# Loop order on TensorE: one V projection ahead of the values calls, one turn of queries behind a projection

## The chip, the cores and the metric

One NeuronCore of a Trainium2 chip runs the whole program. The metric is device time in microseconds of one execution; before the change it is 2621.0 us, the median of three runs.

## The reference

Eight sequences of 1024 tokens with 128 channels pass through a "macaron" block: half a local transformer, full causal attention, half the same local transformer again, each with a layer norm ahead and a residual around it.

```python
x = x + 0.5 * ffn(layernorm(x), ...)
x = x + attn(layernorm(x), Wk, Wq, Wv)
x = x + 0.5 * ffn(layernorm(x), ...)
```

`ffn` has two layers. Each shifts half of the channels by one token, projects to queries, keys and values of 8 heads of 64, normalises queries and keys and rotates them, attends in windows of 64 keys plus the 64 before them, projects back, and then applies a layer norm and a gated feed-forward of 341 hidden units, both with residuals. So local layers run four times in all over every token, and full attention once.

## The kernel before

The work of a local layer is cut into turns of 256 tokens, t = 0 to 127 over the four layers (32 a layer, 64 a phase; phase 0 lies ahead of the full attention and phase 1 behind it). Each turn has two halves i = 0, 1 of 128 tokens. Its steps on TensorE are: `project(t, i, x)`, three matmuls of 512 columns for x = Q, K or V (lines 619 to 621); `turn(t, i, x)`, four transposes of the rotated queries or keys (line 628); `scores(t, i)`, the mask (line 644) and 16 small products of queries and keys (line 652) for score groups 2i and 2i + 1; `turn_p(t, g)`, four transposes of the weights of group g (line 662); `values(t, i)`, 16 products of values and weights (line 678); `wo`, the output projection (lines 690 to 692). Two turns make a pair u, and the feed-forward works on pairs: `turn_rows` (line 701), `turn_back` (718), `to_gate` and `to_up` (723 to 725), `down` (742). `turn_ln` (756) exists in layers 0 and 2 only, `turn_y` (766) in layers 1 and 3 only.

Each engine has its own list of calls, written out by hand. In the middle of each phase the list is a loop, `local`, whose round s issues calls of several turns at different stages, with t = 2s; phase 0 runs s = 9 to 31 and phase 1 runs s = 41 to 62, 45 rounds together. Other engines serve these calls: ScalarE squares projections (line 4395), copies turned queries (4419) and values (4430), takes exponentials group by group (`exp_rows`, 4440, four ACTIVATE with a read of the sum behind each), copies turned weights (4447) and copies the outputs of the values calls (`split_o`, 4454, once for each half). VectorE takes row maxima and rotates, GpSimd adds, scales and normalises.

Results of TensorE lie in eight PSUM banks, each shared by several uses. `ROTA` lists the users of each bank in the order of a round, as (name, lag): the call of turn 2s - lag (or pair s - lag). `FIRST_USERS` and `LAST_USERS` hold the same for the calls outside the loop. From these lists each use gets the one before it in its bank, and `vacant` makes a TensorE call wait until that one has been emptied:

```python
        def vacant(on, what, n):
            before = BEFORE[what, n]
            if before:
                for done in emptied[before[0]]:
                    on.wait_ge(done, emptied_at(*before))
```

Bank 5, which `project(t - 2, 0, V)` writes, is listed as `[("TK0", 3), ("S0", 3), ("V0", 2), ("K0", 1), ("S1", 2), ("G2", 3)]`: ahead of V0 of turn t - 2 comes S0 of turn t - 3, score group 0, which is emptied by its exponentials (semaphore `exped`).

Of the kernel before, what the change touches and what calls it, by code (L numbers as in the profile page):

```python
# [30 lines left out]
Q, K, V = 0, 1, 2  # L31
# [19 lines left out]
    [("Q0", 2), ("YR", 3), ("TQ0", 2), ("K1", 1), ("O1", 3), ("NR", 1)],  # L51
# [10 lines left out]
        [("V1", 0), ("TK0", 0), ("S0", 0), ("TK1", 1), ("O0", 0), ("V1", 2), ("TK0", 2), ("S0", 2), ("P2", 1),  # L62
         ("TK1", 3), ("O0", 2), ("V1", 4), ("TK0", 4), ("S0", 4), ("P2", 3), ("G0", 0), ("TK1", 5), ("W2", 0),
         ("O0", 4), ("V1", 6), ("TK0", 6), ("S0", 6), ("P2", 5), ("G0", 1), ("W2", 1), ("TK1", 7), ("O0", 6), ("V1",
         8), ("TK0", 8), ("S0", 8), ("P2", 7), ("G0", 2), ("W2", 2), ("TK1", 9), ("O0", 8), ("V1", 10), ("TK0", 10),
         ("S0", 10), ("P2", 9), ("G0", 3), ("W2", 3), ("TK1", 11), ("O0", 10), ("V1", 12), ("TK0", 12), ("S0", 12),
         ("P2", 11), ("G0", 4), ("W2", 4), ("TK1", 13), ("O0", 12), ("V1", 14), ("TK0", 14), ("S0", 14), ("P2", 13),
         ("G0", 5)],
        [("Q0", 0), ("TQ0", 0), ("K1", 1), ("NR", 1), ("Q0", 2), ("TQ0", 2), ("K1", 3), ("O1", 1), ("NR", 3),
         ("Q0", 4), ("YR", 0), ("TQ0", 4), ("K1", 5), ("O1", 3), ("NR", 5), ("Q0", 6), ("YR", 1), ("TQ0", 6), ("K1",  # L70
         7), ("O1", 5), ("NR", 7), ("Q0", 8), ("YR", 2), ("TQ0", 8), ("K1", 9), ("O1", 7), ("NR", 9), ("Q0", 10),
         ("YR", 3), ("TQ0", 10), ("K1", 11), ("O1", 9), ("NR", 11), ("Q0", 12), ("YR", 4), ("TQ0", 12), ("K1", 13),
         ("O1", 11), ("NR", 13), ("Q0", 14), ("YR", 5), ("TQ0", 14), ("K1", 15), ("O1", 13), ("NR", 15)],
        [("K1", 0), ("Q0", 1), ("TQ0", 1), ("K1", 2), ("O1", 0), ("Q0", 3), ("WO", 0), ("TQ0", 3), ("K1", 4),
         ("O1", 2), ("Q0", 5), ("WO", 1), ("TQ0", 5), ("K1", 6), ("O1", 4), ("Q0", 7), ("WO", 2), ("TQ0", 7), ("K1",
         8), ("O1", 6), ("Q0", 9), ("WO", 3), ("TQ0", 9), ("K1", 10), ("O1", 8), ("Q0", 11), ("WO", 4), ("TQ0", 11),
# [5 lines left out]
         ("LT", 12), ("V1", 11), ("P1", 10), ("TQ1", 11), ("NR", 12), ("P0", 11), ("Q1", 13), ("LT", 14), ("V1",  # L82
         13), ("P1", 12), ("TQ1", 13), ("NR", 14), ("P0", 13), ("Q1", 15), ("LT", 16)],
        [("V0", 1), ("S3", 0), ("P0", 0), ("P3", 0), ("S3", 1), ("V0", 3), ("S3", 2), ("P0", 2), ("P3", 2), ("S3",
         3), ("V0", 5), ("S3", 4), ("P0", 4), ("P3", 4), ("S3", 5), ("V0", 7), ("S3", 6), ("P0", 6), ("P3", 6),
         ("S3", 7), ("V0", 9), ("S3", 8), ("P0", 8), ("P3", 8), ("S3", 9), ("V0", 11), ("S3", 10), ("P0", 10),
         ("P3", 10), ("S3", 11), ("V0", 13), ("S3", 12), ("P0", 12), ("P3", 12), ("S3", 13), ("V0", 15), ("S3", 14)],
        [("V0", 0), ("K0", 1), ("S1", 0), ("TK0", 1), ("S0", 1), ("V0", 2), ("K0", 3), ("S1", 2), ("TK0", 3),
         ("S0", 3), ("V0", 4), ("K0", 5), ("S1", 4), ("G2", 0), ("TK0", 5), ("S0", 5), ("V0", 6), ("K0", 7), ("S1",
         6), ("G2", 1), ("TK0", 7), ("S0", 7), ("V0", 8), ("K0", 9), ("S1", 8), ("G2", 2), ("TK0", 9), ("S0", 9),  # L90
         ("V0", 10), ("K0", 11), ("S1", 10), ("G2", 3), ("TK0", 11), ("S0", 11), ("V0", 12), ("K0", 13), ("S1", 12),
         ("G2", 4), ("TK0", 13), ("S0", 13), ("V0", 14), ("K0", 15), ("S1", 14), ("G2", 5)],
        [("LT", 1), ("Q1", 0), ("TQ1", 0), ("S2", 0), ("LT", 3), ("P2", 0), ("Q1", 2), ("TQ1", 2), ("O0", 1),
         ("S2", 2), ("LT", 5), ("P2", 2), ("Q1", 4), ("HB", 0), ("TQ1", 4), ("O0", 3), ("S2", 4), ("LT", 7), ("P2",
         4), ("Q1", 6), ("HB", 1), ("TQ1", 6), ("O0", 5), ("S2", 6), ("LT", 9), ("P2", 6), ("Q1", 8), ("HB", 2),
         ("TQ1", 8), ("O0", 7), ("S2", 8), ("LT", 11), ("P2", 8), ("Q1", 10), ("HB", 3), ("TQ1", 10), ("O0", 9),
         ("S2", 10), ("LT", 13), ("P2", 10), ("Q1", 12), ("HB", 4), ("TQ1", 12), ("O0", 11), ("S2", 12), ("LT", 15),
         ("P2", 12), ("Q1", 14), ("HB", 5), ("TQ1", 14), ("O0", 13), ("S2", 14)],
        [("K0", 0), ("TK1", 0), ("K0", 2), ("S1", 1), ("S2", 1), ("TK1", 2), ("P1", 1), ("P3", 1), ("K0", 4),
         ("S1", 3), ("S2", 3), ("TK1", 4), ("P1", 3), ("P3", 3), ("G1", 0), ("K0", 6), ("S1", 5), ("S2", 5), ("TK1",  # L100
         6), ("P1", 5), ("P3", 5), ("G1", 1), ("K0", 8), ("S1", 7), ("S2", 7), ("TK1", 8), ("P1", 7), ("P3", 7),
         ("G1", 2), ("K0", 10), ("S1", 9), ("S2", 9), ("TK1", 10), ("P1", 9), ("P3", 9), ("G1", 3), ("K0", 12),
         ("S1", 11), ("S2", 11), ("TK1", 12), ("P1", 11), ("P3", 11), ("G1", 4), ("K0", 14), ("S1", 13), ("S2", 13),
         ("TK1", 14), ("P1", 13), ("P3", 13), ("G1", 5)],
# [4 lines left out]
         ("W2", 32), ("O0", 68), ("V1", 70), ("TK0", 70), ("S0", 70), ("P2", 69), ("G0", 33), ("W2", 33), ("TK1",  # L109
         71), ("O0", 70), ("V1", 72), ("TK0", 72), ("S0", 72), ("P2", 71), ("G0", 34), ("W2", 34), ("TK1", 73),  # L110
         ("O0", 72), ("V1", 74), ("TK0", 74), ("S0", 74), ("P2", 73), ("G0", 35), ("W2", 35), ("TK1", 75), ("O0",
         74), ("V1", 76), ("TK0", 76), ("S0", 76), ("P2", 75), ("G0", 36), ("W2", 36), ("TK1", 77), ("O0", 76),
         ("V1", 78), ("TK0", 78), ("S0", 78), ("P2", 77), ("G0", 37)],
        [("Q0", 64), ("TQ0", 64), ("K1", 65), ("NR", 65), ("Q0", 66), ("TQ0", 66), ("K1", 67), ("O1", 65), ("NR",
         67), ("Q0", 68), ("YR", 32), ("TQ0", 68), ("K1", 69), ("O1", 67), ("NR", 69), ("Q0", 70), ("YR", 33),
         ("TQ0", 70), ("K1", 71), ("O1", 69), ("NR", 71), ("Q0", 72), ("YR", 34), ("TQ0", 72), ("K1", 73), ("O1",
         71), ("NR", 73), ("Q0", 74), ("YR", 35), ("TQ0", 74), ("K1", 75), ("O1", 73), ("NR", 75), ("Q0", 76),
         ("YR", 36), ("TQ0", 76), ("K1", 77), ("O1", 75), ("NR", 77), ("Q0", 78), ("YR", 37), ("TQ0", 78), ("K1",
         79), ("O1", 77), ("NR", 79)],
        [("K1", 64), ("Q0", 65), ("TQ0", 65), ("K1", 66), ("O1", 64), ("Q0", 67), ("WO", 32), ("TQ0", 67), ("K1",  # L120
         68), ("O1", 66), ("Q0", 69), ("WO", 33), ("TQ0", 69), ("K1", 70), ("O1", 68), ("Q0", 71), ("WO", 34),
         ("TQ0", 71), ("K1", 72), ("O1", 70), ("Q0", 73), ("WO", 35), ("TQ0", 73), ("K1", 74), ("O1", 72), ("Q0",
         75), ("WO", 36), ("TQ0", 75), ("K1", 76), ("O1", 74), ("Q0", 77), ("WO", 37), ("TQ0", 77), ("K1", 78),
         ("O1", 76), ("Q0", 79), ("WO", 38)],
        [("LT", 64), ("NR", 64), ("Q1", 65), ("LT", 66), ("V1", 65), ("P1", 64), ("TQ1", 65), ("NR", 66), ("P0",
         65), ("Q1", 67), ("LT", 68), ("V1", 67), ("P1", 66), ("TQ1", 67), ("NR", 68), ("P0", 67), ("Q1", 69),
         ("LT", 70), ("V1", 69), ("P1", 68), ("TQ1", 69), ("NR", 70), ("P0", 69), ("Q1", 71), ("LT", 72), ("V1",
         71), ("P1", 70), ("TQ1", 71), ("NR", 72), ("P0", 71), ("Q1", 73), ("LT", 74), ("V1", 73), ("P1", 72),
         ("TQ1", 73), ("NR", 74), ("P0", 73), ("Q1", 75), ("LT", 76), ("V1", 75), ("P1", 74), ("TQ1", 75), ("NR",
         76), ("P0", 75), ("Q1", 77), ("LT", 78), ("V1", 77), ("P1", 76), ("TQ1", 77), ("NR", 78), ("P0", 77),  # L130
         ("Q1", 79), ("LT", 80)],
        [("V0", 65), ("S3", 64), ("P0", 64), ("P3", 64), ("S3", 65), ("V0", 67), ("S3", 66), ("P0", 66), ("P3",
         66), ("S3", 67), ("V0", 69), ("S3", 68), ("P0", 68), ("P3", 68), ("S3", 69), ("V0", 71), ("S3", 70), ("P0",
         70), ("P3", 70), ("S3", 71), ("V0", 73), ("S3", 72), ("P0", 72), ("P3", 72), ("S3", 73), ("V0", 75), ("S3",
         74), ("P0", 74), ("P3", 74), ("S3", 75), ("V0", 77), ("S3", 76), ("P0", 76), ("P3", 76), ("S3", 77), ("V0",
# [6423 lines left out]
```

## Time and profile before

| | |
|---|---|
| runs | 2620.84, 2621.0, 2624.25 us; median 2621.0 |
| profiled execution, span | 2623.2 us (the page gives no other time for it) |
| busy | TensorE 98%, VectorE 91%, ScalarE 89%, GpSimd 78% of the span |
| chain that ended last | TensorE 83%, GpSimd 6%, VectorE 5%, ScalarE 4% |

The page's busy line says how much of the span each engine is at work. The timeline lists an engine's instructions in order of time, alike ones merged, with start, length, and the idle time ahead and what ended it. Instructions of one engine overlap in these rows, so the length of one is more than the distance to the next start.

### The profile page before, as it was taken

What the parts mean: (1) busy time and instruction counts of PE and PEld (TensorE: products, weight loads), DVE (VectorE), ACT (ScalarE), POOL (GpSimd) and SP (SyncE); (2) the same over time, 40 slices, a digit from 0 to 9 for tenths busy, and PEclk for the clock granted to TensorE, in tenths of its full rate; (3) what the DMA queues carried; (4) which work ended last, traced back from release to release, by engine and by line L of the source; (5) the groups of instructions that cost most, each with busy time, mean ns of one, the idle gap of its engine ahead of it and who ended that gap; (6) DMA issues with size and microseconds to landing.
All of it is one profiled execution on the core that took longest, in us unless ns stands there. A gap on an engine that the chain in (4) does not pass through costs nothing.

```text
span 2623.2 us, 80275 instructions
## 1 busy us (share of the span) xinstructions
PE 2558.0 (98%) x29132; PEld 2063.6 (79%) x29132; DVE 2376.0 (91%) x6206; ACT 2346.8 (89%) x7379; POOL 2056.4 (78%) x2185
## 2 busy tenths in 40 slices
PE   5999999999999999998999999999999999999998
PEld 4778777877788888886997777778777788888876
DVE  7999999999999999996888999999998999999995
ACT  5999999999999999995555999999999999999996
POOL 7999999988887877872104999999988888787873
PEclk8999999999999999999999999999999999999999
DMA  4121111111111111110000111111111111111110
GB/s 105 44 51 31 28 38 31 28 28 39 24 32 28 28 42 26 32 28 8 9 1 11 32 28 32 26 38 32 29 24 39 28 32 40 30 40 36 36 40 26
DMA packets 63810, 83.95 MB, mean 32 GB/s; under 512 B 11538, under 2 KB 30652, under 8 KB 63420
## 3 DMA queue, kind: packets, MB, share of 16 engines
q1 hardware_dynamic: 63420, 78.82, 13.1%
q8 instruction: 236, 3.87, 0.6%
q14 instruction: 154, 1.26, 0.2%
HBM read 11.67 MB, written 4.19 MB: 6 GB/s over the span
## 4 chain that ended last, share of the span: by engine, by line
PE 83%; POOL 6%; DVE 5%; ACT 4%; issue 2%; SPq 0%; DMA 0%; ACTq 0%; POOLq 0%; DVEq 0%
PE PS L678 8%; PE PS L662 8%; PE PS L628 7%; PE PS L652 7%; PE PS L619 6%; PE PS L742 6%; PE PS L621 6%; PE PS L620 6%; PE PS L723 4%; PE PS L725 3%; PE PS L724 3%; PE PS L644 3%; PE PS L690 2%; PE PS L853 2%; PE PS L692 2%
## 5 line engine op out<-in xcount | busy, mean ns | idle before, releaser
L4440 ACT ACTIVATE P<-PS,MX 128x128 f32<-128x128 f32 x2048 | 754.3, 430 | 2.1 <-DVE MX L2248 1.2
L5756 POOL TENSOR_TENSOR T<-T,SQ 128x512 f32<-128x512 f32 x512 | 652.1, 1284 | 115.3 <-DVE SQ L2209 111.7
L5792 POOL TENSOR_TENSOR P<-P,RI 128x512 f32<-128x512 f32 x512 | 527.8, 1042 | 73.8 <-DVE RI L2254 71.7
L4440 ACT ACTIVATION_READ_ACCUMULATOR P<-PS,MX 128x1 f32 x2048 | 535.6, 268 | 0.0
L5769 POOL TENSOR_TENSOR T<-T,RN 128x512 f32<-128x512 f32 x512 | 525.9, 1048 | 6.2 <-DVE RN L2242 3.8
L2190 DVE TENSOR_REDUCE SS<-SQ 128x8 f32<-128x512 f32 x512 | 343.8, 681 | 44.6 <-ACT SQ L4395 37.9
L4395 ACT ACTIVATE SQ<-PS 128x512 f32<-128x512 f32 x512 | 338.1, 662 | 45.9 <-PE PS L621 35.0
L619 PE MATMUL PS<-WH,YH 128*128 128x512 f32 x768 | 346.1, 451 | 6.9 <-POOL YL L5745 3.3
L2248 DVE TENSOR_REDUCE MX<-PS 128x4 f32<-128x512 f32 x512 | 345.8, 678 | 6.5 <-PE PS L652 6.3
L2209 DVE TENSOR_TENSOR SQ<-PS,TAB 128x512 f32<-128x512 f32 x512 | 349.1, 682 | 2.3
L2201 DVE TENSOR_TENSOR T<-PS,TAB 128x512 f32<-128x512 f32 x512 | 344.2, 682 | 7.1 <-PE PS L628 3.3
L4447 ACT COPY PT<-PS 128x512 f32<-128x512 f32 x512 | 301.9, 626 | 32.1 <-PE PS L662 32.0
L628 PEld LDWEIGHTS PS<-CST,T 128*128 128x128 f32 x2048 | 238.6, 141 | 88.8 <-issue 54.8
L628 PE MATMUL PS<-CST,T 128*128 128x128 f32 x2048 | 292.4, 275 | 14.0 <-POOL T L5769 13.4
L621 PE MATMUL PS<-WH,YL 128*128 128x512 f32 x768 | 305.3, 397 | 0.0
L620 PE MATMUL PS<-WL,YH 128*128 128x512 f32 x768 | 303.4, 395 | 0.0
L662 PE MATMUL PS<-CST,P 128*128 128x128 f32 x2048 | 296.4, 278 | 3.1 <-POOL P L5792 1.0
L678 PEld LDWEIGHTS PS<-PT,VP 128*64 128x64 f32 x8192 | 249.5, 138 | 28.3 <-issue 28.1
L662 PEld LDWEIGHTS PS<-CST,P 128*128 128x128 f32 x2048 | 229.2, 141 | 52.4 <-issue 22.9
L652 PE MATMUL PS<-KT,QT 64*64 64x128 f32 x8192 | 268.6, 269 | 0.0
L678 PE MATMUL PS<-PT,VP 128*64 128x64 f32 x8192 | 267.3, 224 | 0.0
L652 PEld LDWEIGHTS PS<-KT,QT 64*64 64x64 f32 x8192 | 243.4, 133 | 16.9
(155 smaller groups left out, 5938.4 us busy)
## 6 DMA issues: line engine op xcount, KB each, us to landing
VP<-VP SPq DMA_DIRECT2D x480, 128.0 KB, 2.3
out_dram<-X SPq DMA_DIRECT2D x16, 256.0 KB, 2.6
X<-in_L_attn_x_dram SPq DMA_DIRECT2D x7, 512.0 KB, 4.5
SG<-in_L_ffn_w_dram SPq DMA_DIRECT2D x5, 341.0 KB, 3.0
SG<-in_L_ffn_wqkv_dram SPq DMA_DIRECT2D x4, 384.0 KB, 3.4
SGQ<-in_L_ffn_wqkv_dram SPq DMA_DIRECT2D x4, 256.0 KB, 3.5
X<-in_table_dram SPq DMA_DIRECT2D x2, 512.0 KB, 6.5
P<-in_L_ffn_wo_dram SPq DMA_DIRECT2D x2, 256.0 KB, 3.2
```

The source lines that it names most:

```text
L619: pe.matmul(PS[:, b, :], YH[:, k, :], WH[:, cols], start=True, stop=False)
L620: pe.matmul(PS[:, b, :], YH[:, k, :], WL[:, cols], start=False, stop=False)
L621: pe.matmul(PS[:, b, :], YL[:, k, :], WH[:, cols], start=False, stop=True).then_inc(projected[x], 1)
L628: ins = pe.transpose(PS[:, b, 128 * p:128 * p + 128], T1[:, k, 128 * p:128 * p + 128], ident)
L652: ins = pe.matmul(PS[64 * w:64 * w + 64, bank_of(f"S{2 * i + x}", t), 128 * p:128 * p + 128], QT2[at, s, p, m:m + WIN], KT[at, p, k:k + 12 ...
L662: ins = pe.transpose(PS[:, b, 128 * p:128 * p + 128], P[:, g, p, :], ident)
L678: ins = pe.matmul(PS[64 * x:64 * x + 64, b, 128 * p + m:128 * p + m + WIN], VP[:, s, 2 * i + w, d:d + 64], PT[:, 2 * i + x, p, m:m + WIN], ...
L2209: dve.tensor_tensor(SQ[:, (2 * n + 1 - x) % 3, :].rearrange("p (h t d) -> p h t d", h=HEADS, t=2), PS[:, b, :].rearrange("p (h t d) -> p h ...
L4440: ins = act.activation(P[:, g, p, :], PS[:, b, 128 * p:128 * p + 128], ACT.Exp, bias=MX[:, g, p:p + 1], accum_out=SM[:, g, p:p + 1])
L5756: pool.tensor_tensor(T1[:, k, :], T1[:, k, :], SQ[:, (2 * n + 1 - x) % 3, :], ALU.add).then_inc(added[x], 1)
L5769: pool.tensor_tensor(heads, heads, RN[:, t % 2, i, 8 * x:8 * x + 8].unsqueeze(2).broadcast_to([128, HEADS, DH]), ALU.mult).then_inc(scaled ...
L5792: pool.tensor_tensor(P[:, g], P[:, g], RI[:, g, :].unsqueeze(2).broadcast_to([128, NPAIR, 128]), ALU.mult).then_inc(p_scaled, 1)
```

## The change

In `local` on TensorE the projection of queries of turn t - 2 goes ahead of the turn of queries of t - 3, and the projection of values of the first half of t - 2 goes ahead of the two values calls of t - 4.

```diff
                 turn_rows(s - 3)
+                project(t - 2, 1, Q)
                 turn(t - 3, 1, Q)
-                project(t - 2, 1, Q)
                 turn_y(s - 4)
+                project(t - 2, 0, V)
                 values(t - 4, 0)
                 values(t - 4, 1)
-                project(t - 2, 0, V)
                 scores(t - 3, 1)
```

The rest of the diff writes the bank tables with other line breaks. One entry of bank 1 changes, and with it the ends of that bank's lists outside the loop:

```diff
-    [("Q0", 2), ("YR", 3), ("TQ0", 2), ("K1", 1), ("O1", 3), ("NR", 1)],
+    [("NR", 3), ("Q0", 2), ("YR", 3), ("TQ0", 2), ("K1", 1), ("O1", 3)],
```

The lists of the other engines are the same in both kernels. The changed kernel's lines of TensorE stand five higher (619 becomes 614, and so on).

TensorE in a round of layer 1, from turn_rows (L701) to scores (L652), before; L628 is the turn of queries, L766 turn_y, L678 the values calls, and L619 to L621 the projection of queries and then that of values:

```order
L701 MATMUL PS<-CST,Y 128x128 x4
L628 MATMUL PS<-CST,T 128x128 x4
L619 MATMUL PS<-WH,YH 128x512
L620 MATMUL PS<-WL,YH 128x512
L621 MATMUL PS<-WH,YL 128x512
L766 MATMUL PS<-CST,G 128x128 x4
L678 MATMUL PS<-PT,VP 64x64 x32
L619 MATMUL PS<-WH,YH 128x512
L620 MATMUL PS<-WL,YH 128x512
L621 MATMUL PS<-WH,YL 128x512
L644 MATMUL PS<-MLOC,IDB 64x512 x4
L652 MATMUL PS<-KT,QT 64x128 x16
```

And the same place in the changed kernel:

```order
L696 MATMUL PS<-CST,Y 128x128 x4
L614 MATMUL PS<-WH,YH 128x512
L615 MATMUL PS<-WL,YH 128x512
L616 MATMUL PS<-WH,YL 128x512
L623 MATMUL PS<-CST,T 128x128 x4
L761 MATMUL PS<-CST,G 128x128 x4
L614 MATMUL PS<-WH,YH 128x512
L615 MATMUL PS<-WL,YH 128x512
L616 MATMUL PS<-WH,YL 128x512
L673 MATMUL PS<-PT,VP 64x64 x32
L639 MATMUL PS<-MLOC,IDB 64x512 x4
L647 MATMUL PS<-KT,QT 64x128 x16
```

The first projection and the four transposes have changed places, and the second projection now stands between turn_y and the values calls, which come straight ahead of the scores.

TensorE in a round of layer 0, where no turn_y exists, from the turn of queries (before) to the scores, with the semaphores that each call waits for:

```order
L628 MATMUL PS<-CST,T 128x128 [waits p_copied,mul_q]
L628 MATMUL PS<-CST,T 128x128 x3
L619 MATMUL PS<-WH,YH 128x512 [waits p_copied]
L620 MATMUL PS<-WL,YH 128x512
L621 MATMUL PS<-WH,YL 128x512
L678 MATMUL PS<-PT,VP 64x64 [waits k_copied,v_zero,v_moved_even0]
L678 MATMUL PS<-PT,VP 64x64 x15
L678 MATMUL PS<-PT,VP 64x64 [waits cos_k,sin_k,p_copied,v_moved_even1]
L678 MATMUL PS<-PT,VP 64x64 x15
L619 MATMUL PS<-WH,YH 128x512 [waits exped]
L620 MATMUL PS<-WL,YH 128x512
L621 MATMUL PS<-WH,YL 128x512
```

And in the changed kernel:

```order
L614 MATMUL PS<-WH,YH 128x512 [waits p_copied]
L615 MATMUL PS<-WL,YH 128x512
L616 MATMUL PS<-WH,YL 128x512
L623 MATMUL PS<-CST,T 128x128 [waits mul_q]
L623 MATMUL PS<-CST,T 128x128 x3
L614 MATMUL PS<-WH,YH 128x512 [waits exped]
L615 MATMUL PS<-WL,YH 128x512
L616 MATMUL PS<-WH,YL 128x512
L673 MATMUL PS<-PT,VP 64x64 [waits k_copied,v_zero,v_moved_even0]
L673 MATMUL PS<-PT,VP 64x64 x15
L673 MATMUL PS<-PT,VP 64x64 [waits cos_k,sin_k,p_copied,v_moved_even1]
L673 MATMUL PS<-PT,VP 64x64 x15
```

The projection with the wait for `exped` now stands ahead of the values calls, with the same wait; the values calls keep theirs.

## Rows read from the trace of the kernel before

**Rows 1.** The page: span, and busy time with its share of the span.

```profile
span 2623.2 us, 80275 instructions
...
PE 2558.0 (98%) x29132; PEld 2063.6 (79%) x29132; DVE 2376.0 (91%) x6206; ACT 2346.8 (89%) x7379; POOL 2056.4 (78%) x2185
```

**Rows 2.** Timeline of TensorE, round s = 12: start us, us, engine line operation.

```profile
422.03 0.66 PE L662 MATMUL PS<-CST,P 128*128 128x128 f32 x4
422.52 0.60 PE L701 MATMUL PS<-CST,Y 128*128 128x128 f32 x4
422.96 0.60 PE L628 MATMUL PS<-CST,T 128*128 128x128 f32 x4
423.31 0.48 PE L619 MATMUL PS<-WH,YH 128*128 128x512 f32 x1
...
424.19 2.09 PE L678 MATMUL PS<-PT,VP 128*64 128x64 f32 x64
426.20 0.50 PE L619 MATMUL PS<-WH,YH 128*128 128x512 f32 x1
...
427.24 0.41 PE L644 MATMUL PS<-MLOC,IDB 64*64 64x512 bf16 x4
...
428.45 0.50 PE L619 MATMUL PS<-WH,YH 128*128 128x512 f32 x1
```

**Rows 3.** Timeline of ScalarE, the same stretch of round s = 12.

```profile
422.72 0.59 ACT L4447 COPY PT<-PS 128x512 f32<-128x512 f32 x1 [0.34 <-PE PS L662]
...
424.49 0.22 ACT L4440 ACTIVATION_READ_ACCUMULATOR P<-PS,MX 128x1 f32 x1
...
426.82 0.27 ACT L4440 ACTIVATION_READ_ACCUMULATOR P<-PS,MX 128x1 f32 x1
426.91 1.14 ACT L4454 CAST OTH<-PS 128x512 fp32r<-128x512 f32 x2
```

**Rows 4.** Timeline of TensorE, round s = 25, which has turn_y.

```profile
898.06 0.60 PE L701 MATMUL PS<-CST,Y 128*128 128x128 f32 x4
...
899.63 0.60 PE L766 MATMUL PS<-CST,G 128*128 128x128 f32 x4
900.16 2.08 PE L678 MATMUL PS<-PT,VP 128*64 128x64 f32 x64
...
903.12 0.41 PE L644 MATMUL PS<-MLOC,IDB 64*64 64x512 bf16 x4
...
904.33 0.50 PE L619 MATMUL PS<-WH,YH 128*128 128x512 f32 x1
```

**Rows 5.** Timeline of ScalarE, the same stretch of round s = 25.

```profile
900.03 0.22 ACT L4440 ACTIVATION_READ_ACCUMULATOR P<-PS,MX 128x1 f32 x1
...
902.45 1.14 ACT L4454 CAST OTH<-PS 128x512 fp32r<-128x512 f32 x2
...
903.60 0.69 ACT L4430 COPY VP<-PS 128x512 f32<-128x512 f32 x1
```

**Rows 6.** Windows: stretch, length, busy of each engine, PEclk, DMA share, GB/s.

```profile
427.00:438.80 11.80, 11.72 (x130) 9.40 (x130) 11.30 (x32) 11.80 (x43) 11.72 (x14) 1.00 0.21 47
902.50:914.30 11.80, 11.80 (x132) 9.64 (x131) 10.87 (x26) 11.80 (x44) 11.62 (x14) 1.00 0.16 35
```

**Rows 7.** Timelines of ScalarE and TensorE: copy of queries, K projection behind it.

```profile
432.72 0.77 ACT L4419 COPY QT<-PS 128x512 f32<-128x512 f32 x1
...
433.55 0.50 PE L619 MATMUL PS<-WH,YH 128*128 128x512 f32 x1
```

**Rows 8.** Timelines of ScalarE and TensorE: exponentials and turn_p, rounds 12 and 25.

```profile
438.55 0.28 ACT L4440 ACTIVATION_READ_ACCUMULATOR P<-PS,MX 128x1 f32 x1
...
438.98 1.10 PE L662 MATMUL PS<-CST,P 128*128 128x128 f32 x8
...
914.09 0.28 ACT L4440 ACTIVATION_READ_ACCUMULATOR P<-PS,MX 128x1 f32 x1
...
914.51 1.11 PE L662 MATMUL PS<-CST,P 128*128 128x128 f32 x8
```

203 rows, old and new, of tables (FIRST_USERS, LAST_USERS) are left out of this document.

## Prediction

> **What bounds the kernel now.** Read the page's busy line first: TensorE is busy for 98% of the 2623.2 us span, while VectorE and ScalarE stand at 91% and 89% [rows 1]. The page gives that span and no other time of the profiled execution; it lies 2.2 us above the median of the runs shown (2621.0) and inside their range (2620.84 to 2624.25), so the sum below is made against 2623.2 and its difference is put on 2621.0.
>
> TensorE works in order, so moving its calls can only change two things: what it pays between unlike calls, and where it waits. Next therefore the timeline of one round of the loop. There are two kinds. In 22 rounds (s = 9 to 19 and 41 to 51) no turn_y exists; I call them plain. In 23 rounds (s = 20 to 31 and 52 to 62) turn_y(s - 4) stands ahead of the values calls; I call them Y rounds. Within a kind the rounds read alike, so one of each stands for all.
>
> In the plain round the reader is to see that turn_rows starts at 422.52, the turn of queries 0.44 later, the projection of queries 0.35 after that, the two values calls at 424.19, the V projection at 426.20 and scores(t - 3, 1) at 427.24 [rows 2]. On ScalarE the exponentials of score group 0 of turn t - 3 end at 424.49 + 0.22 = 424.71, those of group 1 at 426.82 + 0.27 = 427.09 [rows 3]. The scores call starts 0.15 after that second end: it already waits for ScalarE. So the kernel is not bound by TensorE alone: two engines run in step. From 427.0 to 438.8 and from 902.5 to 914.3 ScalarE is busy for 11.80 of 11.80 us, at a granted TensorE clock of 1.00 [rows 6].
>
> **The change, part by part.** Work, transfers and the order on ScalarE, VectorE, GpSimd and the DMA queues stay as they were. The tables of bank users are only written with other line breaks, and NR's entry goes from the end of a round (lag 1) to the front of the next (lag 3), which is the same turn, hence the same sequence in bank 1: priced at nothing, because no wait is gained or lost.
>
> *The turn of queries goes behind the projection.* In either order the two calls and their surroundings cost the same: before 0.44 (turn_rows) + 0.35 (turn) + 0.78 (projection to transposes: the 1.57 from 898.06 to 899.63 less 0.44 and 0.35), now 0.35 + 0.78 + 0.44 [rows 2, 4]. Who waits for the later turn? ScalarE's copy of these queries, which stands behind the square of the very projection that now goes first, and behind the exponentials that end at 424.71; the turn, which would start at 422.52 + 0.35 + 0.78 = 423.65 and takes 0.60, is done by 424.25. Cost nothing; if that cover went, scores(t - 3, 1) would be late by what is lacking.
>
> *The V projection goes in front of the values calls.* What it is moved past does not matter so much as what it needs. Project(t - 2, 0, V) writes PSUM bank 5, whose user before it is S0 of turn t - 3, so it must wait until the exponentials of group 0 of t - 3 are done. Behind the values calls that was long past (424.71 against 426.20). In front of them it is not. Without a wait it would start at 422.52 + 0.35 + 0.78 + 0.35 = 424.00 in the plain round and at 898.06 + 0.35 + 0.78 + 0.44 + 0.35 = 899.98 in the Y round; the exponentials end at 424.71 and at 900.03 + 0.22 = 900.25 [rows 3, 5]. What a released projection needs after the release is read where one waits now: the copy of queries ends at 432.72 + 0.77 = 433.49 and the K projection behind it starts at 433.55, 0.06 later [rows 7]. So it starts at 424.77 and at 900.31: new waits of 0.77 and 0.33 us. The nearest other row is the scores call, 0.15 after its release; I take 0.06, since it is the same call, and keep 0.15 for the range.
>
> *What is queued behind that wait.* The two values calls. A projection takes 0.88 up to the values calls (423.31 to 424.19), so they start at 425.65 and 901.19 instead of 424.19 and 900.16, and they last 2.09 and 2.08 [rows 2, 4]: they end at 427.74 and 903.27.
>
> Two engines feel this. TensorE itself comes to scores(t - 3, 1) 2.01 after the values start (424.19 to 426.20), at 427.66 and 903.20, against 427.24 and 903.12: late by 0.42 and 0.08. How the change from the 128*64 to the 64*64 form is priced, the trace of before does not show cleanly; a change of form costs 0.09 where it does (transposes to values 0.53 against transposes to transposes 0.44), so it lies between 0 and about 0.1. It matters little, because the other engine decides:
>
> ScalarE copies the two outputs of the values calls one after the other from 426.91 and ends at 426.91 + 1.14 = 428.05 (Y round 902.45 + 1.14 = 903.59) [rows 3, 5]. Now the second copy must wait for the later values call. A copy of this size starts 0.03 after TensorE's row ends (422.03 + 0.66 = 422.69, copy at 422.72) and takes 0.59 when it follows a wait, so it ends at 427.74 + 0.03 + 0.59 = 428.36 and 903.27 + 0.03 + 0.59 = 903.89: ScalarE is late by 0.31 and 0.30 [rows 2, 3].
>
> *Where that ends up.* ScalarE has no idle time for the next 11 us [rows 6], so its lateness stays. In both kinds of round TensorE then waits for it: turn_p(t - 3, 2) starts at 438.98 and 914.51, 0.15 and 0.14 after the exponentials that end at 438.83 and 914.37 [rows 8]. The 0.42 of the plain round is more than 0.31, but part of it is no loss: from the scores call to this turn_p the plain round takes 11.74 and the Y round 11.39 for the same calls, so 0.35 of the plain one is waiting, which a later start eats. What is left is ScalarE's 0.31 and 0.30.
>
> **Sum.** 22 x 0.31 + 23 x 0.30 = 6.8 + 6.9 = 13.7 us: 2623.2 becomes 2636.9, and on the median 2621.0 becomes **2634.7**.
>
> **Rivals.** *A: the late copy is made up.* If ScalarE's 11.80 of 11.80 hides slack (the rows of one engine overlap, so a full stretch can hold short gaps), only TensorE's own lateness counts: 0.42 - 0.35 = 0.07 plain, 0.08 Y; 22 x 0.07 + 23 x 0.08 = 3.4 us, so 2624.4. For it: a copy of the same size in this stretch lasts 0.69 rather than 0.59 [rows 5], so some of what is counted as busy is queueing. Against: TensorE waits for exactly this engine at the end of the stretch in both kinds.
>
> *B: faster.* If no wait held either the V projection or the scores call, the stretch from turn_rows to the second V projection would be 0.35 + 0.78 + 0.35 + 0.88 + 2.01 + 1.21 = 5.58 instead of 428.45 - 422.52 = 5.93, and with turn_y's 0.44 it would be 6.02 instead of 904.33 - 898.06 = 6.27 (1.21 is the scores call, 903.12 to 904.33). That is 22 x 0.35 + 23 x 0.25 = 13.5 us, so 2607.5. It decides only if the exponentials of group 0 end 0.77 (plain) or 0.33 (Y) sooner than they do. They follow the copy at 422.72, which TensorE released just before turn_rows, and nothing ahead of that is moved; that speaks against it. For it: a change of form does cost something, 0.09 as above, and the values and scores calls now stand side by side. The Trainium skill, "TensorEngine Tiling (Array Packing)", section "Tiling Modes", states that a change of tiling mode drains TensorE; there are three changes now where there were four, and by that rule alone, at the row's 0.09, the time would fall by 45 x 0.09 = 4 us, to 2617. The trace agrees that a change costs something, not that it decides here.
>
> *C: the wait costs more.* With 0.15 after the release in place of 0.06, and a second output copy that lasts 0.69, as the copy at 903.60 does, in place of 0.59 [rows 5], each round loses 0.09 + 0.10 more: 45 x 0.19 = 8.6, so 2643.3. For it: the scores call of the same round pays 0.15. Against: the K projection pays 0.06, and a copy after a wait takes 0.59.
>
> That the change does nothing is no rival: the V projection really stands ahead of the values calls, and the wait is in its own order row.
>
> **Chances.** Forecast 0.66, A 0.15, B 0.05, C 0.14. The range holds the forecast and C, 2626 to 2644, with a little room at C for the unknown change of form; A and B, 0.20, are left out. About 0.2%, 5.2 us, is what a measurement of this kernel can tell from no change; A lies inside it. So faster 0.05, same 0.15, slower 0.80.
>
> **What would show it.** After the change: the first V projection of a round starts 0.06 (not 0) after the end of the exponentials of group 0; the values calls start some 1.5 us later after turn_rows in a plain round and 1.0 us in a Y round; the second of the output copies stands apart from the first; both kinds of round grow by 0.30 and the attention stage keeps its length. I am wrong if the V projection does not wait, if the turn_p calls of rows 8 keep their distance from turn_rows, or if the two kinds grow by very different amounts.

## The result, and the profile after

The changed kernel takes 2636.39 us (median of four runs, 2634.85 to 2639.24) against 2622.39 for the kernel before (four runs, 2620.84 to 2624.25): a ratio of 1.0054, 95% interval 1.0042 to 1.0066. It is 14.0 us slower; 13.7 were forecast. The profiled execution has a span of 2637.5 us, 14.3 over the one before [rows 1].

The page, span and busy time: TensorE has 4.6 us more of busy time and a smaller share, so 9.7 of the 14.3 us that were added are time in which it is not busy.

```profile
span 2637.5 us, 80230 instructions
...
PE 2562.6 (97%) x29132; PEld 2064.5 (78%) x29132; DVE 2378.7 (90%) x6206; ACT 2347.4 (89%) x7379; POOL 2054.5 (78%) x2185
```

The groups by line say where. Columns: line, engine, operation, names, shapes, count | busy us, mean ns | idle time before the group in us, with what ended it. First the copies of outputs (ScalarE) and the first matmul of a projection (TensorE) in the kernel before:

```profile
L4454 ACT CAST OTH<-PS 128x512 fp32r<-128x512 f32 x256 | 160.6, 674 | 3.4 <-PE PS L678 2.8 <-issue 0.3
L619 PE MATMUL PS<-WH,YH 128*128 128x512 f32 x768 | 346.1, 451 | 6.9 <-POOL YL L5745 3.3 <-DVE RN L2242 1.2 <-ACT Y L4505 0.6
```

Then in the changed one:

```profile
L4449 ACT CAST OTH<-PS 128x512 fp32r<-128x512 f32 x256 | 164.7, 657 | 13.6 <-PE PS L673 13.1 <-issue 0.3
L614 PE MATMUL PS<-WH,YH 128*128 128x512 f32 x768 | 347.4, 452 | 19.2 <-ACT P L4435 11.5 <-POOL YL L5740 3.1 <-ACT Y L4500 0.6
```

A projection now waits for ScalarE's exponentials (11.5 us), and the copies of outputs wait for the values calls: 13.6 - 3.4 = 10.2 us more, which is 45 rounds of 0.23. These are idle times between rows, and rows of one engine overlap; how late a call comes is read from starts and ends below.

One plain round, s = 12, on TensorE (timeline: start us, us, engine line operation, idle time ahead and what ended it); it answers to [rows 2] and, in its last line, to [rows 8]:

```profile
424.67 0.60 PE L696 MATMUL PS<-CST,Y 128*128 128x128 f32 x4
...
426.91 0.50 PE L614 MATMUL PS<-WH,YH 128*128 128x512 f32 x1 [0.52 <-ACT P L4435]
...
427.80 2.09 PE L673 MATMUL PS<-PT,VP 128*64 128x64 f32 x64
429.81 0.41 PE L639 MATMUL PS<-MLOC,IDB 64*64 64x512 bf16 x4
...
441.41 1.10 PE L657 MATMUL PS<-CST,P 128*128 128x128 f32 x8
```

And on ScalarE, which answers to [rows 3]:

```profile
426.63 0.22 ACT L4435 ACTIVATION_READ_ACCUMULATOR P<-PS,MX 128x1 f32 x1
...
429.05 0.65 ACT L4449 CAST OTH<-PS 128x512 fp32r<-128x512 f32 x1
429.93 0.58 ACT L4449 CAST OTH<-PS 128x512 fp32r<-128x512 f32 x1 [0.23 <-PE PS L673]
430.41 0.30 ACT L4379 CAST YH<-Y 128x128 fp32r<-128x128 f32 x1
```

The exponentials of group 0 end at 426.85, the V projection starts 0.06 later, the values calls stand 3.13 after turn_rows, and the two copies, one merged row in [rows 3], stand apart with an idle gap between them. The Y round, s = 25, on TensorE (it answers to [rows 4]) and on ScalarE ([rows 5]):

```profile
903.99 0.60 PE L696 MATMUL PS<-CST,Y 128*128 128x128 f32 x4
...
906.23 0.50 PE L614 MATMUL PS<-WH,YH 128*128 128x512 f32 x1
...
907.12 2.08 PE L673 MATMUL PS<-PT,VP 128*64 128x64 f32 x64
909.13 0.41 PE L639 MATMUL PS<-MLOC,IDB 64*64 64x512 bf16 x4
...
920.73 1.11 PE L657 MATMUL PS<-CST,P 128*128 128x128 f32 x8
```

```profile
909.25 0.59 ACT L4449 CAST OTH<-PS 128x512 fp32r<-128x512 f32 x1 [0.23 <-PE PS L673]
```

In both kinds turn_p(t - 3, 2) stands 16.74 after turn_rows, where it stood 16.46 and 16.45 [rows 2, 4, 8].

The length of a round is the distance from one turn_rows to the next; s = 12 and 25 stand for their kinds, in us:

| kernel | plain | Y | added, plain and Y | time against before (95% interval) |
|---|---|---|---|---|
| before | 36.83 | 36.40 | | |
| the change | 37.12 | 36.68 | 0.33 and 0.31 | 1.0054 (1.0042 to 1.0066) |
| E1, only Q | 36.84 | 36.40 | 0.01 and 0.00 | 1.0002 (0.9993 to 1.0011) |
| E2, only V | 37.12 | 36.68 | 0.33 and 0.31 | 1.0048 (1.0034 to 1.0062) |
| E3, V between | 36.79 | 36.67 | 0.00 and 0.30 | 1.0032 (1.0019 to 1.0044) |
| E4, cast first | 36.92 | 36.49 | 0.13 and 0.12 | 1.0030 (1.0019 to 1.0041) |
| E5, V ahead of turn_y | 37.11 | 37.12 | 0.32 and 0.75 | 1.0091 (1.0077 to 1.0105) |
| E6, no wait | 36.81 | 36.37 | 0.02 and 0.00 | 1.0034 (1.0022 to 1.0047) |
| E7, copy waits | 36.80 | 36.59, later 36.37 | 0.01 and 0.22 | 1.0002 (0.9993 to 1.0011) |
| F1, four buffers | 36.61 | 36.34 | -0.18 and -0.03 | 0.9972 (0.9961 to 0.9983) |

The ten profiles have two paces. The round s = 5 lies outside the loops, where the calls keep their order; it takes 36.84 in the profiles of before and of E1 and 36.79 in the others (36.95 in E6, whose banks differ there). So what an edit adds is counted against rounds of the same pace that it doesn't touch: 36.79 for a plain round and 36.37, the later rounds of E7, for a Y round; E1 is counted against before. The prediction held that the rounds of a kind read alike. That is not so for s = 16 to 19 and 48 to 51, around the change of layers: they take 36.38 to 37.05 before. The change adds 0.3 to 0.4 there too.

From turn_rows of the first to that of the last round of both loops the change takes 12.3 us more than the profile before, and 13.7 more than E7 without its six longer rounds, which has the change's pace. These are 43 rounds; with the two that are missing it is about 14.4 (22 x 0.33 + 23 x 0.31), where the runs measured 14.0. The full attention, from its first matmul to its last values call, keeps its 197.8 us. Single executions differ by more than what is left between these sums: up to round s = 5, where nothing was moved, the ten of the table take 161.4 to 165.4 us.

### The profile page after: what moved, and what is told of

It is laid out like the page before. It is cut to its first block, busy times and chain, and to the rows that moved or that the text cites. A ratio compares the mean times of both kernels' runs of the same rounds, so it can differ in the third digit from the quotient of the medians.

```text
span 2637.5 us, 80230 instructions
## 1 busy us (share of the span) xinstructions
PE 2562.6 (97%) x29132; PEld 2064.5 (78%) x29132; DVE 2378.7 (90%) x6206; ACT 2347.4 (89%) x7379; POOL 2054.5 (78%) x2185
## 4 chain that ended last, share of the span: by engine, by line
PE 88%; ACT 7%; issue 2%; DVE 2%; POOL 1%; DMA 0%; SPq 0%; ACTq 0%; DVEq 0%; POOLq 0%
PE PS L673 9%; PE PS L657 9%; PE PS L647 8%; PE PS L623 7%; PE PS L614 7%; PE PS L737 6%; PE PS L616 6%; PE PS L615 6%; ACT P L4435 4%; PE PS L718 4%; PE PS L720 3%; PE PS L719 3%; PE PS L639 3%; PE PS L685 3%; PE PS L848 2%; PE PS L687 2%
## 5 line engine op out<-in xcount | busy, mean ns | idle before, releaser
L4435 ACT ACTIVATION_READ_ACCUMULATOR P<-PS,MX 128x1 f32 x2048 | 528.0, 260 | 0.0
L4390 ACT ACTIVATE SQ<-PS 128x512 f32<-128x512 f32 x512 | 332.1, 650 | 48.4 <-PE PS L616 37.5
L614 PE MATMUL PS<-WH,YH 128*128 128x512 f32 x768 | 347.4, 452 | 19.2 <-ACT P L4435 11.5
```

Of the source, the lines that this page charges most:

```text
L614: pe.matmul(PS[:, b, :], YH[:, k, :], WH[:, cols], start=True, stop=False)
L4435: ins = act.activation(P[:, g, p, :], PS[:, b, 128 * p:128 * p + 128], ACT.Exp, bias=MX[:, g, p:p + 1], accum_out=SM[:, g, p:p + 1])
```

## The experiments

The order on TensorE after turn_rows is, before, turn Q, project Q, turn_y, values, values, V, scores. The edits of E1 to E5 are made to the changed kernel.

**E1 and E2: the two parts apart.** E1 keeps only the swap of queries, E2 only the V projection.

```diff
 E1
-                project(t - 2, 0, V)
                 values(t - 4, 0)
                 values(t - 4, 1)
+                project(t - 2, 0, V)
 E2
-                project(t - 2, 1, Q)
                 turn(t - 3, 1, Q)
+                project(t - 2, 1, Q)
```

> Only the turn of queries goes behind the projection; the V projection stays behind the values calls. Theory (the wait of the V projection, carried by ScalarE's late second output copy, is all of it): no change, 2622.4 within 2 us; both kinds of round keep 36.79 and 36.41 us. Rival (the swap of turn and projection has a share, for instance through the copy of queries): part of the 14 us stays, 2626 or more.

> Only the V projection goes in front of the values calls; turn and projection of queries stand as before. Theory: the V projection waits for the same exponentials, so it starts at the same place (2.25 us after turn_rows) and all of the 14 us stays, 2636 within 2 us. Rival (two parts of the change share the cost): clearly under 2634.

E1 is where the kernel before is, in its time and in both kinds of round, and it has the change's bank tables too; E2 is where the change is, 1.0048. The idle time ahead of the copies, in groups by line, is 3.3 us in E1 and 13.8 in E2 (before 3.4, change 13.6). The swap of queries and the tables cost nothing; the V projection is all of it.

**E3: the V projection between the values calls.**

```diff
-                project(t - 2, 0, V)
                 values(t - 4, 0)
+                project(t - 2, 0, V)
                 values(t - 4, 1)
```

> The V projection stands between the two values calls. TensorE then comes to scores(t - 3, 1) no later than before (4.62 against 4.72 us after turn_rows in a plain round, 5.05 against 5.06 in a Y round), but the second values call ends 0.93 us later than before. Theory (the second output copy carries it): in a plain round that call is done at 4.72, before ScalarE wants it at 4.86: no loss. In a Y round it is done at 5.15, so the copy starts 0.3 late, of which about 0.1 is eaten by the wait for the K projection that the Y round has already: Y rounds 0.2 longer, plain rounds as before, 23 x 0.2 = 4.6 us, about 2627. Rival (lateness of TensorE at the scores carries it): no change in either kind, 2622. Rival (a V projection in front of a values call costs in itself): both kinds longer by about 0.3, 2636.

The plain rounds are as long as untouched ones, the Y rounds 0.30 longer where 0.2 was expected, and the time is 2632.09 us, 8.4 over before, where 4.6 was expected (23 rounds of 0.30 are 6.9). So a V projection ahead of a values call costs nothing by itself: it does where it makes the copy late. ScalarE in the plain round of E3 has the two copies in one row, as before; in the Y round they stand apart:

```profile
426.58 1.13 ACT L4449 CAST OTH<-PS 128x512 fp32r<-128x512 f32 x2
...
903.25 0.65 ACT L4449 CAST OTH<-PS 128x512 fp32r<-128x512 f32 x1
904.13 0.58 ACT L4449 CAST OTH<-PS 128x512 fp32r<-128x512 f32 x1 [0.23 <-PE PS L673]
```

TensorE in the same Y round shows why the expectation was short (turn_rows at 898.87):

```profile
900.97 1.15 PE L673 MATMUL PS<-PT,VP 128*64 128x64 f32 x32
902.05 0.50 PE L614 MATMUL PS<-WH,YH 128*128 128x512 f32 x1
...
902.93 1.15 PE L673 MATMUL PS<-PT,VP 128*64 128x64 f32 x32
904.01 0.41 PE L639 MATMUL PS<-MLOC,IDB 64*64 64x512 bf16 x4
```

The values calls, parted, take 1.08 each up to the next call, so the scores start 5.14 after turn_rows instead of 5.05, and the copy 0.41 late instead of 0.3. It ends 904.13 + 0.58 - 898.87 = 5.84 after turn_rows, as in the change. And the 0.1 that I took off for ScalarE's wait for the K projection doesn't come off (see below). In the Y round E3 doesn't part the lateness of TensorE from that of the copy; E4 and E7 do.

**E4: fill ScalarE's gap.**

```diff
                 split_o(t - 12, 0)
-                split_o(t - 12, 1)
                 split_y(t - 9, 1)
+                split_o(t - 12, 1)
```

> The changed order on TensorE, but on ScalarE the 0.2 us cast of normed tokens (split_y) goes ahead of the second output copy, so that 0.2 of the 0.4 us in which ScalarE waits for the values call is filled. Theory: what follows the copy on ScalarE is late by 0.2 instead of 0.41 at its start; TensorE's own lateness (0.42 plain, 0.09 Y at the scores) now shows through the square of the K projection: 0.1 to 0.2 a plain round, 0.1 a Y round are left of 0.30 and 0.27, so about 5.5 of 14 us, 2628. Rival (the copy on ScalarE is not what carries it): all of it stays, 2636.

TensorE issues as in the change and comes to the scores just as late, but of the 0.33 and 0.31 only 0.13 and 0.12 are left: 0.2 us of work went into the gap, and 0.2 us of the loss are gone. ScalarE in the plain round and in the Y round:

```profile
427.64 0.65 ACT L4449 CAST OTH<-PS 128x512 fp32r<-128x512 f32 x1
428.12 0.37 ACT L4379 CAST YH<-Y 128x128 fp32r<-128x128 f32 x1
428.52 0.58 ACT L4449 CAST OTH<-PS 128x512 fp32r<-128x512 f32 x1
...
904.96 0.37 ACT L4379 CAST YH<-Y 128x128 fp32r<-128x128 f32 x1
905.35 0.58 ACT L4449 CAST OTH<-PS 128x512 fp32r<-128x512 f32 x1
```

The second copy starts as late as in the change (5.27 after turn_rows); what was put into the gap is gone from behind it. Round s of ScalarE's loop serves the values calls of TensorE's round s - 4, so the last four Y rounds of each phase are served by the calls behind ScalarE's loop, which keep the old order: these rounds take 36.68, as in the change, in the same execution. The rival, by which the copy does not matter, falls. The time is 2630.97 us, 7.3 over before, where 5.5 was expected; the Y rounds in the old order have a share in that.

**E5: a larger dose.**

```diff
+                project(t - 2, 0, V)
                 turn_y(s - 4)
-                project(t - 2, 0, V)
                 values(t - 4, 0)
```

> A larger dose in the Y rounds alone: the V projection goes ahead of turn_y as well, so turn_y's 0.53 us, which before lay inside the wait, now comes behind it. Theory: plain rounds as after the change (37.08); in a Y round the values calls go 0.43 later still, the second output copy with them, so a Y round grows by 0.27 + 0.43 = 0.70 over before (37.11). 23 x 0.43 = 9.9 us over the changed kernel, about 24 over before. Rival (TensorE's lateness at the scores is what counts): 0.09 + 0.43 = 0.52 a Y round, 20 over before. Rival (a V projection in front costs in itself, wherever): no more than the 14 of the change.

37.12 a Y round, 0.72 over before (0.70 expected) and 0.75 over an untouched round of its pace, and 23.6 us in all (1.0091). TensorE's 0.52 and the fixed cost fall; the copy's lateness counts. The second copy of the Y round on ScalarE (turn_rows stands at 902.67):

```profile
908.37 0.59 ACT L4449 CAST OTH<-PS 128x512 fp32r<-128x512 f32 x1 [0.29 <-PE PS L673]
```

It ends 6.29 after turn_rows, 0.76 later than before [rows 5].

**E6: the same order, no wait.** V0 and O0 of even turns exchange banks, in ROTA and in the lists outside the loop.

```diff
-    [("W2", 4), ("TK1", 3), ("O0", 4), ("V1", 2), ("TK0", 2), ("S0", 2), ("P2", 3), ("G0", 3)],
+    [("W2", 4), ("TK1", 3), ("V0", 2), ("V1", 2), ("TK0", 2), ("S0", 2), ("P2", 3), ("G0", 3)],
...
-    [("TK0", 3), ("S0", 3), ("V0", 2), ("K0", 1), ("S1", 2), ("G2", 3)],
+    [("TK0", 3), ("S0", 3), ("O0", 4), ("K0", 1), ("S1", 2), ("G2", 3)],
```

> The changed order on TensorE with the wait taken away: for turns of the first kind V0 and O0 exchange banks, so the V projection writes bank 0, whose last user was copied long before, and the first values call writes bank 5 behind score group 0. The V projection then starts at 1.49 us after turn_rows in a plain round and 1.92 in a Y round instead of 2.25; the values calls are 0.76 and 0.33 earlier, the second one done at 4.5 and 4.9, so ScalarE's copy at 4.86 is late by nothing in a plain round and by under 0.1 in a Y round. New: the second V projection waits for the copy of the first (6.23 + 0.06), 0.35 late against before in a plain round, which the square of the K projection shows as 0.1, and 0.02 in a Y round. Theory (the wait is the cost): about 0.1 a plain round and 0.05 to 0.1 a Y round, 3 to 5 us over before instead of 14. Rival (the order costs in itself, by changes of form or by the place of the values calls): 12 us or more over before.

TensorE in the plain round of E6:

```profile
424.75 0.60 PE L710 MATMUL PS<-CST,Y 128*128 128x128 f32 x4
...
426.23 0.48 PE L628 MATMUL PS<-WH,YH 128*128 128x512 f32 x1
...
427.10 2.08 PE L687 MATMUL PS<-PT,VP 128*64 128x64 f32 x64
429.45 0.41 PE L653 MATMUL PS<-MLOC,IDB 64*64 64x512 bf16 x4 [0.27 <-ACT P L4449]
...
431.01 0.50 PE L628 MATMUL PS<-WH,YH 128*128 128x512 f32 x1 [0.27 <-ACT VP L4439]
```

The V projection starts 1.48 after turn_rows (1.92 in the Y round), against 2.24 in the change: that is TensorE's wait, 0.76 and 0.32. The scores wait for their exponentials again, and both kinds of round are as short as untouched ones; the 0.05 to 0.1 that I expected did not come. The order without its wait costs nothing in the loop, and saves nothing: what TensorE saves in the plain round is spent waiting for ScalarE, at the scores and at the next V projection. As a whole E6 is still 8.3 us over before (1.0034; 3 to 5 were expected, inside the loops). This loss lies outside the loops. There the old order, values calls ahead of the V projection, meets the exchanged banks, and the values calls wait for the exponentials instead: 0.60 in a round such as s = 5, and in s = 64:

```profile
2551.37 2.08 PE L687 MATMUL PS<-PT,VP 128*64 128x64 f32 x64 [1.74 <-ACT P L4449]
```

The rounds with the old order (s = 3 to 8, 32, 33, 36 to 40, 63 to 65) take 5.2 us more than in the profile before; the profiled execution, 2629.84 us, is the fastest of the five.

**E7: the late copy alone.** The edit is to the kernel before; TensorE's order isn't touched.

```diff
             on.wait_ge(valued, TPC * t + i + 1)
+            if i == 1 and t % 2 == 0 and t < TURN - 16:
+                on.wait_ge(projected[V], TPC * (t + 2) + 1)
             act.copy(OTH[:, :, 128 * i:128 * i + 128],
```

> The order before on TensorE, but ScalarE's second output copy also waits until the V projection (project(t - 2, 0, V)) is done. In a plain round that is at 4.66, ahead of the copy at 4.86: nothing. In a Y round at 5.09: the copy starts 0.26 late, and nothing on TensorE is moved. Theory (the late copy alone makes the round longer, less the 0.11 in which ScalarE of a Y round waits for the K projection anyway): Y rounds 0.14 longer, plain rounds as before, 3 us in all. Rival (ScalarE makes a late copy up, or TensorE has to be late too): both kinds as before.

The edit's bound on t ends the wait at turn 48, so only the Y rounds s = 20 to 25 have it, and s = 26 to 31 and 52 to 62 are a control in the same execution. That is why the whole time doesn't show it. Rounds 25 and 26 on ScalarE, the merged row of both copies and the cast behind them (turn_rows at 896.53 and 933.12):

```profile
900.91 1.37 ACT L4456 CAST OTH<-PS 128x512 fp32r<-128x512 f32 x2
902.18 0.30 ACT L4384 CAST YH<-Y 128x128 fp32r<-128x128 f32 x1
...
937.50 1.14 ACT L4456 CAST OTH<-PS 128x512 fp32r<-128x512 f32 x2
938.45 0.40 ACT L4384 CAST YH<-Y 128x128 fp32r<-128x128 f32 x1
```

With the wait the two copies end 5.75 after turn_rows, without it 5.52; the cast ends at 5.95 and 5.73. So ScalarE's results are 0.22 to 0.23 late. The scores stand at 5.05 in both, so TensorE is not late there. The rounds take 36.59 and 36.37, 0.22 longer, where 0.14 was expected. A late copy alone makes the round longer, by its whole lateness.

**F1: a faster kernel.** The gap in which ScalarE waits for turn_p(t - 4, 3) is 0.34 us [rows 3]. A cast of 0.2 us that stands behind the output copies fits into it, once the rings of normed tokens have a fourth buffer. The edit is to the kernel before; ring indices change from % 3 to % 4 throughout.

```diff
-    YH = sb("YH", [3, 128], F32R)
-    YL = sb("YL", [3, 128], F32R)
+    YH = sb("YH", [4, 128], F32R)
+    YL = sb("YL", [4, 128], F32R)
...
-                on.wait_ge(projected[x], n - 2)
+                on.wait_ge(projected[x], n - 3)
...
                 split_o(t - 12, 1)
-                split_y(t - 9, 1)
+                if s == ROUNDS[phase][0]:
+                    split_y(t - 9, 1)
...
                 copy_k(t - 9, 1)
+                if s + 1 < ROUNDS[phase][1]:
+                    split_y(t - 7, 1)
                 copy_p(t - 10, 3)
```

> A try for a faster kernel, on the order before: the high and low parts of the normed tokens get four buffers in place of three, and ScalarE's 0.2 us cast of the next round goes from behind the output copies into the 0.5 to 0.77 us in which ScalarE waits for turn_p(t - 4, 3). Theory (from turn_rows to turn_p(t - 3, 2) ScalarE bounds the plain rounds, TensorE the Y rounds): plain rounds 0.1 to 0.2 shorter, Y rounds as before, 2 to 4 us faster. Rival (ScalarE bounds both): 0.2 in both, 9 us. Rival (TensorE bounds both): nothing.

2614.81 us, 0.9972 of the kernel before (0.9961 to 0.9983): 7 us faster where 2 to 4 were expected, and by the medians faster than the change by 21.6. Plain rounds are 0.18 to 0.20 shorter than untouched ones of the same pace, Y rounds 0.03. From the first to the last turn_rows of the loops it is 4.8 us faster than E7 with its six longer rounds taken out; rounds s = 7, 8 and 37 to 40, outside TensorE's loops, gain 0.2 each as well, since ScalarE's loop serves them too. That plain rounds gain the whole 0.2 says that there the time hangs on ScalarE. In Y rounds the gain ends where ScalarE waits for TensorE's K projection: the copy ahead of its square ends 0.18 sooner than in E7's later rounds, the square starts at 7.97 after turn_rows in both. ScalarE ahead of a plain round (turn_rows at 418.98):

```profile
418.68 0.34 ACT L4384 CAST YH<-Y 128x128 fp32r<-128x128 f32 x1
419.18 0.59 ACT L4447 COPY PT<-PS 128x512 f32<-128x512 f32 x1 [0.16 <-PE PS L662]
```

The copy of turned weights starts 0.20 after turn_rows as before; the cast ahead of it is paid out of the gap, which is now 0.16.

## Why the prediction was right

**The order alone costs nothing in the loops, the Q swap nothing.** E6 and E1 show both.

**The wait.** 0.06 after the release was taken from the K projection; the V projection pays 0.06 after the row's end in the plain round. Forecast 2.25 after turn_rows, measured 2.24 in both kinds; values calls 3.13, measured 3.13; scores 5.14, measured 5.14.

**The copy.** Forecast: its end 0.31 and 0.30 later. Measured: 429.93 + 0.58 - 424.67 = 5.84 and 909.25 + 0.59 - 903.99 = 5.85, against 5.53 before [rows 2 to 5]: 0.31 and 0.32.

**Where it ends up.** Forecast: 0.31 and 0.30 at turn_p(t - 3, 2); measured 0.28 and 0.29 against the profile before, and the rounds grew by 0.29 and 0.28. That profile has the slower pace. At the change's own pace the rounds grew by 0.33 and 0.31, which is 14.4 us for the forecast's 13.7 and the measured 14.0.

**That the lateness stays was right; that ScalarE does not wait was not.** I held that ScalarE has no idle time for 11 us behind the copies, because its rows filled 11.80 of 11.80 us [rows 6]. It does wait there, in both kernels, and the overlapping rows hide it. In the plain round the exponential behind NH starts 0.04 and 0.03 after VectorE's row maxima (MX) end. VectorE before and in the changed kernel:

```profile
436.47 0.18 DVE L2254 RECIPROCAL RI<-SM 128x4 f32<-128x4 f32 x1 [0.34 <-ACT P L4440]
436.56 0.66 DVE L2248 TENSOR_REDUCE MX<-PS 128x4 f32<-128x512 f32 x1
```

```profile
438.90 0.18 DVE L2249 RECIPROCAL RI<-SM 128x4 f32<-128x4 f32 x1 [0.34 <-ACT P L4435]
439.00 0.66 DVE L2243 TENSOR_REDUCE MX<-PS 128x4 f32<-128x512 f32 x1
```

ScalarE before, in rounds 12 and 25:

```profile
427.86 0.40 ACT L4384 CAST YH<-Y 128x128 fp32r<-128x128 f32 x1
...
436.48 0.95 ACT L4481 ACTIVATE NH<-PS,COLS 128x512 fp32r<-128x512 f32 x1
437.26 0.44 ACT L4440 ACTIVATE P<-PS,MX 128x128 f32<-128x128 f32 x1
...
905.46 0.71 ACT L4430 COPY VP<-PS 128x512 f32<-128x512 f32 x1
906.03 0.64 ACT L4395 ACTIVATE SQ<-PS 128x512 f32<-128x512 f32 x1
```

And in the changed kernel:

```profile
439.02 0.85 ACT L4476 ACTIVATE NH<-PS,COLS 128x512 fp32r<-128x512 f32 x1
439.69 0.43 ACT L4435 ACTIVATE P<-PS,MX 128x128 f32<-128x128 f32 x1
...
911.79 0.61 ACT L4425 COPY VP<-PS 128x512 f32<-128x512 f32 x1
912.25 0.65 ACT L4390 ACTIVATE SQ<-PS 128x512 f32<-128x512 f32 x1
```

The wait makes nothing up, because VectorE is late by as much: its row maxima stand behind a reciprocal that waits for ScalarE's own exponentials (idle 0.34 in both) and starts 13.95 after turn_rows before, 14.23 now. In the Y round before, the square waits for the K projection and starts 0.57 after the copy ahead of it, in the change 0.46; there too the ends are as late behind the wait as ahead of it.

How late ScalarE is has to be taken from ends of rows, for these release the other engines (the V projection starts 0.06 after one). By starts it looks as if some 0.1 were made up: the cast YH starts 0.40 late (5.74 after turn_rows for 5.34), the exponential 0.28 and the square 0.29. By ends the cast is 0.30 late, NH 0.29, the exponential 0.27, and copy and square of the Y round 0.30 each. Rows that follow others closely begin sooner and last longer: the cast lasts 0.40 before and 0.30 behind the gap. The Trainium skill, "Perfetto Trace Analysis", section "Per-instruction lifecycle: what the profiler-reported window actually captures", says that a row of ScalarE ends when its write is acknowledged; the trace agrees so far as rows begin before the one ahead has ended (before, the cast at 427.86, the copies' row ends at 428.05 [rows 3]). So a full stretch is no proof that the engine never waits.

The other doses agree on the size, each by the end of ScalarE's late row: 0.23 late and 0.22 longer in E7, 0.76 late and 0.75 longer in E5.

**The rivals.** A, the late copy is made up, gave 3.4 us by TensorE's own lateness alone. It is refuted: E4 gets 0.2 a round back when 0.2 of ScalarE's gap is filled, with TensorE as late as in the change, and E7 loses 0.22 with TensorE on time. B needed the wait to be absent; E6 makes it absent and saves nothing in the loops, since in the plain round the scores and the next V projection then wait for ScalarE. C's dearer wait did not come: 0.06, and the second copy takes 0.58.

## What to carry to other kernels

Before a call is moved ahead, ask which engine empties its buffer, and then who copies the result of the calls that it now holds up: the cost was not TensorE's wait of 0.76 or 0.32 but the 0.33 or 0.31 by which ScalarE's results came later. A stretch in which an engine's rows fill all the time can hide waits; take lateness from the ends of rows, against a round of the same execution that the edit doesn't touch, not from busy time. And where an engine that bounds a stretch has a gap elsewhere in the round, a call moved into that gap, here for one more buffer, is worth its whole length in the rounds that this engine bounds (0.2), and little in the others (0.03).

## What was not expected of the hardware

Parting a pair of values calls costs: both together take 2.01 us to the next call (427.80 to 429.81 in the change), parted they take 1.08 each in the Y round of E3, 0.15 more for the pair. And the pace differs a little between executions: from turn_rows to turn_p(t - 3, 2) the undisturbed plain round takes 16.45 in the profiles of before and of E1, and 16.42 in those of E3, E6 and E7. It isn't the edits, since round s = 5, which the change does not touch, shows it too (36.84 before, 36.79 in the change); in that round ScalarE's rows fall behind evenly, by 0.01 us in the first 5 and 0.03 in 16. What makes it is not shown. Differences of 0.03 a round between two profiles therefore say nothing unless they are set against untouched rounds.
